# An attention and channel-mix block on one core: the slots of its later stages are renumbered, and VectorE takes short stages of the last step

## The reference

```python
x = x + layernorm(attention(layernorm(x), w_qkv, out_w, out_b))
x = x + layernorm(channel_mix(layernorm(x), W_r, W_k, W_v, mu_r, mu_k))

# attention:   q, k, v = split(x @ w_qkv); softmax(q @ k.T / 16) @ v @ out_w.T + out_b
# channel_mix: x_prev = x one row earlier (zeros ahead of the first row of a batch)
#              xr = mu_r * x + (1 - mu_r) * x_prev;  xk = mu_k * x + (1 - mu_k) * x_prev
#              sigmoid(xr @ W_r.T) * (relu(xk @ W_k.T) ** 2 @ W_v.T)
# x is (4, 2048, 256) fp32; attention runs over the 2048 rows of its batch, with one head of 256
```

## Time and profile before

| | |
|---|---|
| three runs | 866.08, 867.44 (median), 869.02 us |
| the profiled execution | 871.26 us, span 869.5 us |
| busy, share of the span | TensorE 815.0 us (94%), VectorE 677.2 (78%), ScalarE 506.0 (58%), GpSimd 490.7 (56%) |
| chain that ended last | TensorE 75%, VectorE 17%, ScalarE 2%, GpSimd 1% |

### The profile page before, as it was taken

One profiled execution on the slowest core, in us unless ns is written; L12 is line 12 of the kernel. 1 busy time (PEld: TensorE's weight loads), 2 busy tenths in 40 slices (PEclk: granted clock), 3 DMA queues, 4 the chain that ended last, 5 costly groups with the idle time before them and its releaser, 6 DMA issues.

```text
span 869.5 us, 16121 instructions
## 1 busy us (share of the span) xinstructions
PE 815.0 (94%) x5870; PEld 614.5 (71%) x5870; DVE 677.2 (78%) x1755; ACT 506.0 (58%) x638; POOL 490.7 (56%) x650
## 2 busy tenths in 40 slices
PE   4779999999999999999999999999999999999854
PEld 3447767777777777777777777777777777777843
DVE  4687897877898888878898888887877777787741
ACT  3264655765565756655565666556665665556442
POOL 1100345656665675566556756665567656667864
PEclk9989999999999999999999999999999999999967
DMA  6559747445555637464745656445544554446001
GB/s 177 108 115 174 160 112 143 107 107 137 116 120 130 150 85 165 97 140 100 132 115 134 141 122 140 122 105 121 114 106 99 108 107 113 116 92 155 29 24 37
DMA packets 336574, 101.58 MB, mean 117 GB/s; under 512 B 310256, under 2 KB 336240, under 8 KB 336496
## 3 DMA queue, kind: packets, MB, share of 16 engines
q1 hardware_dynamic: 336496, 100.56, 52.1%
HBM read 18.75 MB, written 8.39 MB: 31 GB/s over the span
## 4 chain that ended last, share of the span: by engine, by line
PE 75%; DVE 17%; issue 2%; ACT 2%; POOL 1%; DMA 1%; SPq 1%; DVEq 0%; POOLq 0%; ACTq 0%
PE M L795 6%; PE M L796 6%; PE M L797 6%; PE S L827 5%; PE S L831 5%; PE S L828 5%; PE S L830 5%; PE S L829 5%; PE Y L846 5%; PE Y L850 5%; PE Y L848 5%; PE Y L849 5%; PE Y L847 5%; DVE p_lo L664 4%; DVE probs L648 3%
## 5 line engine op out<-in xcount | busy, mean ns | idle before, releaser
L648 DVE TENSOR_SCALAR_CACHE_REDUCE probs<-S 128x512 f32<-128x512 f32 x256 | 174.9, 685 | 116.0 <-PE S L831 113.4
L481 ACT ACTIVATE probs<-probs,exp_bias,kappa 128x2048 f32<-128x2048 f32 x64 | 134.1, 2095 | 174.9 <-DVE exp_bias L659 174.9
L664 DVE TENSOR_TENSOR p_lo<-probs,p_hi 128x2048 f16<-128x2048 f32 x64 | 171.1, 2674 | 2.5 <-ACT p_hi L442 2.4
L846 PE MATMUL Y<-pt_hi,planes 128*128 128x256 f16 x512 | 139.6, 273 | 1.5 <-issue 1.5
L850 PE MATMUL Y<-pt_hi,planes 128*128 128x256 f16 x512 | 139.6, 273 | 0.0
L848 PE MATMUL Y<-pt_hi,planes 128*128 128x256 f16 x512 | 139.6, 273 | 0.0
L849 PE MATMUL Y<-pt_lo,planes 128*128 128x256 f16 x512 | 139.6, 273 | 0.0
L847 PE MATMUL Y<-pt_lo,planes 128*128 128x256 f16 x512 | 139.5, 273 | 0.0
L442 ACT ACTIVATE p_hi<-probs 128x2048 f16<-128x2048 f32 x64 | 122.1, 1907 | 1.0
L827 PE MATMUL S<-turned,q_hi 128*128 128x512 f16 x256 | 99.6, 389 | 9.5 <-DVE probs L648 7.4
L403 POOL TENSOR_TENSOR xm_lo<-mixed,xm_hi 128x512 fp32r<-128x512 f32 x64 | 82.5, 1308 | 35.1 <-ACT xm_hi L442 35.1
(11 more groups left out here) (128 smaller groups left out, 2034.0 us busy)
## 6 DMA issues: line engine op xcount, KB each, us to landing
x_res<-in_L_attn_x SPq DMA_DIRECT2D x32, 256.0 KB, 3.1
out_x<-gate SPq DMA_DIRECT2D x32, 256.0 KB, 2.6
xs<-in_L_attn_x SPq DMA_DIRECT2D x32, 128.0 KB, 3.0
xs<-in_L_attn_x SPq DMA_DIRECT2D x16, 256.0 KB, 3.9
pt_hi<-p_hi SPq DMA_TRANSPOSE x64, 3.7
pt_lo<-p_lo SPq DMA_TRANSPOSE x64, 3.7
pt_hi<-in_L_attn_weight_qkv SPq DMA_DIRECT2D x3, 128.0 KB, 2.9
pt_hi<-in_L_attn_weight_qkv SPq DMA_DIRECT2D x1, 256.0 KB, 3.2
```

Of the source, the lines that this page charges most:

```text
L648: dve.tensor_scalar(probs[:, t, c * BLK:(c + 1) * BLK], S[k % RING][:, :], 1.0, None, ALU.mult, ALU.max, accum_out=chunk_max[:, t, c:c + 1 ...
L664: dve.tensor_tensor(p_lo[:, t, :], probs[:, t, :], p_hi[:, t, :], ALU.subtract).then_inc(p_lo_made, 1)
L846: pe.matmul(to[:, 0, :], low, p_h, start=first, stop=False, skip_group_check=True)
```

## The change

The table of slots is written anew. HIGH, LOWER and TURN_P of the first tile move one slot back (5, 6, 6 to 6, 7, 7), VALUES from 13 to 15, Y_HIGH and Y_LOW from 21 and 22 to 23, PROJECT and ATTEND from 23 and 24 to 25, RES_RSQRT from 29 to 31, TURN from 32 to 33 (in a steady step it now stands right behind PROJECT in its slot), RECEPT and KEYS from 41 and 42 to 42, SQUARE from 43 to 44, RECEPT_OUT from 43 to 45, FEED from 46 to 47. QUERY goes forward from -5 to -6, GATE_NORM from 55 to 49, FINISH from 56 to 50, STORE from 57 to 55. ATTEND, MIX_IN, MIX and GATE keep their order; MIX_IN stays at 31 and GATE at 47. The slots of the first step's exponents (FIRST_EXP and the like) stay. And for the last step alone (`DRAIN = H - 1`), ATT_NORM and GATE_NORM leave ScalarE, and RESIDUAL, DIFF, SPLIT_LOW, SQUARE_LOW and FINISH leave GpSimd; VectorE does them. Its norms take mean and rstd directly, so in that step GpSimd leaves out the two operations that make the shift.

```diff
-    VALUES = 13
+    VALUES = 15
...
-    Y_HIGH, Y_LOW, PROJECT = 21, 22, 23
+    Y_HIGH = 23
+    Y_LOW = 23
+    PROJECT = 25
...
+    DRAIN = H - 1
...
@@ att_rsqrt (GpSimd); gate_rsqrt has the same edit with g for a
-                pool.tensor_tensor(aminus[:, :], zeros[:, :], amv[:, :, 0], ALU.subtract).then_inc(a_mean_turned, 1)
+                if h < DRAIN:
+                    pool.tensor_tensor(aminus[:, :], zeros[:, :], amv[:, :, 0], ALU.subtract).then_inc(a_mean_turned, 1)
...
-                pool.wait_ge(a_rstd_made, h + 1)
-                pool.wait_ge(a_mean_turned, h + 1)
-                pool.tensor_tensor(ashift[:, :], aminus[:, :], arstd[:, :], ALU.mult).then_inc(a_shift_made, 1)
+                if h < DRAIN:
+                    pool.wait_ge(a_rstd_made, h + 1)
+                    pool.wait_ge(a_mean_turned, h + 1)
+                    pool.tensor_tensor(ashift[:, :], aminus[:, :], arstd[:, :], ALU.mult).then_inc(a_shift_made, 1)
...
@@ GpSimd's loop; FINISH, SPLIT_LOW and RESIDUAL likewise, ATT_NORM and GATE_NORM in ScalarE's
-                if (h := at(k, SQUARE_LOW)) is not None:
+                if (h := at(k, SQUARE_LOW)) is not None and h < DRAIN:
                     squares_low(h)
                 if (h := at(k, DIFF)) is not None:
-                    differences(h)
+                    if h < DRAIN:
+                        differences(h)
                     carry(h)
...
@@ VectorE: add_attention, differences, split_low, squares_low and finish as GpSimd has them, and
+            def attention_norm(h):
+                dve.wait_ge(a_rstd_made, h + 1)
+                for t in range(RT):
+                    o = att[:, h % 2, t, :]
+                    dve.tensor_scalar(o, o, amv[:, t, 0:1], arstd[:, t:t + 1], ALU.subtract, ALU.mult).then_inc(att_normed, 1)
...
@@ VectorE's loop, between ATTEND and GATE, and behind GATE_STATS
+                if (h := at(k, ATT_NORM)) is not None and h >= DRAIN:
+                    attention_norm(h)
+                if (h := at(k, RESIDUAL)) is not None and h >= DRAIN:
+                    add_attention(h)
+                if (h := at(k, DIFF)) is not None and h >= DRAIN:
+                    differences(h)
+                if (h := at(k, SPLIT_LOW)) is not None and h >= DRAIN:
+                    split_low(h)
+                if (h := at(k, SQUARE_LOW)) is not None and h >= DRAIN:
+                    squares_low(h)
...
+                if (h := at(k, GATE_NORM)) is not None and h >= DRAIN:
+                    gate_norm(h)
+                if (h := at(k, FINISH)) is not None and h >= DRAIN:
+                    finish(h)
```

More of the change, by code:

```diff
@@ L45, in sandwich @@
     EXP = (4, 8)
-    HIGH = (5, 9)
-    LOWER = (6, 10)
-    FIRST_EXP, FIRST_HIGH, FIRST_LOWER = (7, 8), (7, 9), (7, 10)
-    TURN_P = (6, 10)
-    INVERT = 11
-    VALUES = 13
-    LOAD_RES = 18
-    Y_HIGH, Y_LOW, PROJECT = 21, 22, 23
-    ATTEND, ATT_RSQRT, ATT_NORM, RESIDUAL = 24, 25, 26, 27
-    RES_STATS, RES_RSQRT, MIX_IN, TURN = 28, 29, 31, 32
-    XT, DIFF, MIX, SPLIT, SPLIT_LOW = 34, 35, (36, 37), 38, 38
-    RECEPT, KEYS, RECEPT_OUT, SQUARE, SQUARE_LOW, FEED = 41, 42, 43, 43, 44, 46
-    GATE, GATE_STATS, GATE_RSQRT, GATE_NORM, FINISH, STORE = 47, 49, 50, 55, 56, 57
-    QUERY, Q_HIGH, Q_LOW = -5, -4, -3
+    HIGH = (6, 9)
+    LOWER = (7, 10)
+    FIRST_EXP = (7, 8)
+    FIRST_HIGH = (7, 9)
+    FIRST_LOWER = (7, 10)
+    TURN_P = (7, 11)
+    INVERT = 10
+    VALUES = 15
+    LOAD_RES = 17
+    Y_HIGH = 23
+    Y_LOW = 23
+    PROJECT = 25
+    ATTEND = 25
+    ATT_RSQRT = 26
+    ATT_NORM = 26
+    RESIDUAL = 27
+    RES_STATS = 28
+    RES_RSQRT = 31
+    MIX_IN = 31
+    TURN = 33
+    XT = 33
+    DIFF = 33
+    MIX = (36, 37)
+    SPLIT = 39
+    SPLIT_LOW = 39
+    RECEPT = 42
+    KEYS = 42
+    RECEPT_OUT = 45
+    SQUARE = 44
+    SQUARE_LOW = 44
+    FEED = 47
+    GATE = 47
+    GATE_STATS = 48
+    GATE_RSQRT = 48
+    GATE_NORM = 49
+    FINISH = 50
+    STORE = 55
+    QUERY = -6
+    Q_HIGH = -6
+    Q_LOW = -3
     PREP, PREP_EVERY = 10, 12
@@ L426, in _ @@
                     res_rsqrt(h)
-                if (h := at(k, RESIDUAL)) is not None:
+                if (h := at(k, RESIDUAL)) is not None and h < DRAIN:
                     add_attention(h)
                 if (h := at(k, DIFF)) is not None:
-                    differences(h)
+                    if h < DRAIN:
+                        differences(h)
                     carry(h)
-                if (h := at(k, SPLIT_LOW)) is not None:
+                if (h := at(k, SPLIT_LOW)) is not None and h < DRAIN:
                     split_low(h)
@@ L435, in _ @@
                     pre_rsqrt(n)
-                if (h := at(k, FINISH)) is not None:
+                if (h := at(k, FINISH)) is not None and h < DRAIN:
                     finish(h)
@@ L555, in _ @@
                     probs_high(*ht)
-                if (h := at(k, ATT_NORM)) is not None:
+                if (h := at(k, ATT_NORM)) is not None and h < DRAIN:
                     attention_norm(h)
@@ L567, in _ @@
                     query_high(h)
-                if (h := at(k, GATE_NORM)) is not None:
+                if (h := at(k, GATE_NORM)) is not None and h < DRAIN:
                     gate_norm(h)
@@ L729, in gated_stats, with add_attention, differences, split_low @@
                     dve.bn_aggr(gmv[:, t, :], gst[:, t, :]).then_inc(g_moments, 1)
+            def add_attention(h):
+                dve.wait_ge(res_in[h % 2], (h // 2 + 1) * 16)
+                if h >= 4:
+                    dve.wait_ge(out_made, (h - 3) * RT)
+                for t in range(RT):
+                    dve.wait_ge(att_normed, h * RT + t + 1)
+                    dve.tensor_tensor(res[:, h % 4, t, :], x_res[:, h % 2, t, :], att[:, h % 2, t, :],
+                                       ALU.add).then_inc(res_made, 1)
+            def differences(h):
+                dve.wait_ge(xt_made, h + 1)
+                dve.wait_ge(carried, h + 1)
+                dve.tensor_tensor(diff[:, :, :], xt[:, h % 2, :, 1:ROWS + 1], xt[:, h % 2, :, 0:ROWS],
+                                   ALU.subtract).then_inc(diff_made, 1)
+            def split_low(h):
+                for i in range(2):
+                    dve.wait_ge(xm_hi_made, h * 2 + i + 1)
+                    dve.tensor_tensor(xm_lo[:, i], mixed[:, i], f32(xm_hi[:, i]), ALU.subtract).then_inc(xm_lo_made, 1)
+            def squares_low(h):
+                dve.wait_ge(sq_made, h + 1)
+                dve.wait_ge(sq_hi_made, h + 1)
+                dve.tensor_tensor(sq_lo[:, :, :], square[:, :, :], f32(sq_hi[:, :, :]), ALU.subtract).then_inc(sq_lo_made, 1)
+            def finish(h):
+                for t in range(RT):
+                    dve.wait_ge(g_normed, h * RT + t + 1)
+                    dve.tensor_tensor(gate[:, h % 2, t, :], gate[:, h % 2, t, :], res[:, h % 4, t, :],
+                                       ALU.add).then_inc(out_made, 1)
+            def attention_norm(h):
+                dve.wait_ge(a_rstd_made, h + 1)
+                for t in range(RT):
+                    o = att[:, h % 2, t, :]
+                    dve.tensor_scalar(o, o, amv[:, t, 0:1], arstd[:, t:t + 1], ALU.subtract, ALU.mult).then_inc(att_normed, 1)
+            def gate_norm(h):
+                dve.wait_ge(g_rstd_made, h + 1)
+                for t in range(RT):
+                    o = gate[:, h % 2, t, :]
+                    dve.tensor_scalar(o, o, gmv[:, t, 0:1], grstd[:, t:t + 1], ALU.subtract, ALU.mult).then_inc(g_normed, 1)
             pre_stats_of(0)
```

9 lines of the change are left out of this document (5 added, 4 removed).

## The result

The changed kernel took 856.54 us as the median of 4 runs (854.79 to 856.65), the kernel before 868.23 on the same chip (4 runs, 866.08 to 870.77): ratio 0.9851, 95% interval 0.9829 to 0.9873 (the two medians alone give 0.9865, inside it). Run again twice, beside later experiments, it gave 0.9835 (0.9807 to 0.9863) and 0.9857 (0.9838 to 0.9876). The forecast was 852 with a range of 847 to 861. The profiled execution took 856.61 us (span 854.8), 14.65 us less than that of before. The sum of the prediction was 15.5, or 855.8 on that basis.

A forecast was written before the change was run, and what follows sets the result against it. TensorE bounds the steady part, a chain of short stages the drain. Start 2.9, steady 8.2 and drain 4.4 sum to 15.5 us, taken from the median 867.4: 851.9, forecast 852, range 847 to 861 for eight in ten.

The forecast's parts named there:

- rival (1): Steady part and drain: VectorE and GpSimd locks keep half the ten waits or half the drain's gain; 856 to 861, chance 0.20.
- Part 1: Steady steps: all ten waits of TURN for MIX_IN go, 8.2 us; at the worst end 0.
- Part 2: Start: both QUERYs move ahead of TensorE's waits for copies of scores and are hidden, 2.9 us, bounds 1 and 4.3.
- Part 3: Drain: the new order and VectorE's stages shorten the chain of the last steps, 4.4 us, bounds 1 and 8.
- (a): Drain, last values: most of their transfer wait stays, but the stall ahead of FEED(28) goes, 0.9 us.
- (b): Drain, ScalarE ahead of FEED(29): KEYS(29)'s result is taken sooner, 1.9 us, and 0.3 for GpSimd's order.
- rival (2): Drain: the clock stays up behind the wait there, 3 to 5 us more; 847 to 849, chance 0.09.
- (c): Drain, MIX_IN of step 31: no longer beside GpSimd's FINISH(29), but perhaps beside SPLIT_LOW(30); 0.4 of 0.8 us.
- (d): Drain, step 31's DIFF, SPLIT_LOW and SQUARE_LOW moved from GpSimd to VectorE: 0.2 us in the sum.
- (e): Tail of the drain: last norms and additions on VectorE take 1.7 us instead of 2.4, a gain of 0.7.
- additions of over 0.7 us each on VectorE: Last step in the drain: a sign that would show the drain's forecast gain of 4.4 us wrong.
- Rival (4): Every step: VectorE's chain makes MIX_IN late, from 1.8 us delay over the count; 870 to 880, chance 0.07.

The follow-up runs named there:

- E3: The kernel before with one number changed, TURN in slot 33 instead of 32; ratio to before 0.9906.
- E5: The changed kernel with TURN back in slot 32 instead of 33; ratio to before 1.0620.
- E9: The kernel before with TURN at 33, QUERY and Q_HIGH at -6, and VectorE taking the last step's stages except SQUARE_LOW; ratio to before 0.9852.
- E8: The changed kernel with GATE_NORM and FINISH of steps 28 and 29 at slot 52, step 30's and SPLIT_LOW of 30 and 31 on VectorE; ratio to before 0.9816.

## Why the prediction was right, step by step

The mechanism of the steady part is shown (E3, E5). That the sum came so near is in part luck: its three terms of 2.9, 8.2 and 4.4 us measured 0.6, 8.1 and 6.0 in the profiled execution, so a start that was too high and a drain that was too low cancel. And 856.54 lies 0.5 us outside the forecast's own band (849 to 856), in that of rival (1) (856 to 861), though what rival (1) tells did not happen: none of the ten waits stayed, and the drain gave more than forecast.

- **Part 1, the steady steps, 8.2 us: right, by two errors that cancel.** The mechanism is as told: MIX_IN ends 7.3 to 8.25 us after slot 7's start (predicted 7.5 to 8.2), TURN is reached at 9.34 (9.3), and no wait for ATTEND's bank or for copies has come in. E3 and E5 show that TURN's slot decides. But the ten waits were worth 9.2, not 8.2 us: I added 0.16 us to each for the part that a drawn-out matmul hides, and the runs show 0.26. Against it stands that the new table's step is longer, 24.55 instead of 24.49 us (E3, E9), some 1.7 us over the 27.4 steps between units 36 and 255. With 0.4 for the one wait for Y_LOW that also went, 9.2 + 0.4 - 1.7 = 7.9 of the 8.1 measured.
- **Part 2, the start, 2.9 us: mis-sized.** QUERY is hidden as predicted. But in the first and the third execution the units of scores behind the two waits run at half clock, 1.4 to 1.5 us more at each place than in the second, and starting the values later uncovered a wait of 2.50 us at 57.01. The sum had neither. Measured 0.6, 4.0 and 1.1 us in three executions, against one of before: the bounds were 1 and 4.3.
- **Part 3, the drain, 4.4 us: right in direction, 6.0, 4.5 and 5.9 measured in three executions, with one term of the wrong sign.** From the first execution: (a) 1.15 for 0.9. (b) 1.5 for 2.2: the wait ahead of FEED(29) is 3.60, not 3.1 (rival (2) of the prediction reckoned with 4.3 for the same wait, which does not fit its own term). (c) MIX_IN(31) was to win 0.4 and lost 0.6: it met GpSimd's SPLIT_LOW(30), 2.54 us long, and took 2.18. (d) 0.3 for 0.2. (e) 1.2 for 0.7: from the end of the last rstd to the last addition it takes 1.44 us, where 1.7 was predicted and 2.4 was before. What the sum did not have are 2.4 us ahead of FEED(30) and RECEPT(31): there the clock was back up. From first to last matmul KEYS(30) and FEED(30) took 1.30 and 1.40 us, before 2.35 and 2.52, which is 2.2 of the 2.4. The prediction had named additions of over 0.7 us each on VectorE as a sign that this part is wrong; the pair of 1.82 us is that, and the drain gained all the same.
- **Rival (2), the clock.** It came true in part. FEED(29) still paid, FEED(30) did not, and in the second execution FEED(30) paid too. The window answering to the earlier trace rows, then those of FEED(30) and FEED(31), of the changed kernel:

```profile
822.00:824.00 2.00, 2.00 (x9) 2.00 (x10) 1.85 (x8) 0.00 (x0) 0.34 (x1) 0.50 0.17 57
836.00:838.00 2.00, 1.68 (x12) 1.47 (x12) 1.30 (x2) 0.27 (x1) 0.16 (x1) 1.00 0.00 0
845.00:847.00 2.00, 2.00 (x10) 2.00 (x11) 0.00 (x0) 0.00 (x0) 0.00 (x0) 0.52 0.07 21
```

- By the Trainium skill (SBUF — State Buffer, section on who interferes with whom), an operation of VectorE with two inputs in SBUF contends with one of GpSimd that reads SBUF, and in VectorE's two-port modes (both ports for one operand), which tensor_scalar can enter, whoever issues first holds the shared ports for the whole instruction. The pair of additions of 1.82 us, and the pairs of tensor_scalar of 1.54 and 2.18, against 0.73 to 0.75 in E8, agree; the prediction had the hold for the whole length from two-input operations, which the section does not say in so many words. The price I had put on it, 2.0 instead of 4.4 us for the drain, did not come. The one place where the rows show it on the chain is MIX_IN ahead of TURN(31), and E8, where these three pairs are short, ended its span only 0.2 us nearer to unit 255.
- **The basis.** 855.8 from the profiled execution was right to 0.8 us; I forecast 852 from the median of three runs, which was low: over all 50 runs of the kernel before, on several chips, the median is 869.96 (865.29 to 872.86), and over 14 of the changed kernel 856.39. So of the 4.5 us between 852 and 856.54 some 2.5 are the basis, and most of the rest is that the gain by these medians is 13.6 us, not 15.5.
- **Rival (4), slower:** the delay was never near 1.8 us; E5 shows the price beyond it, 2.2 us a step.

What stays open: why the granted clock falls at other places in executions of one kernel, at the start and in the drain; why the start of E9 takes 114.5 us although QUERY is moved there too; and which of the new neighbours lengthens the step by 0.06 us.
